# Up and gate in seven block products, the last product as a stage of its own, and w2's absolute sums through an accumulating DMA

## The reference

```
def wbin(w, base):                      # for (w1, w2, w3)
    d = w - base
    return base + mean(abs(d)) * sign(d)
xn  = layernorm(x2)                     # 1024 rows of 1024
h   = silu(xn @ wbin(w1).T) * (xn @ wbin(w3).T)   # 3584 wide
out = x2 + h @ wbin(w2).T
```

## Time and profile before

| | |
|---|---|
| median of 3 runs | 1373.06 us |
| profiled execution | span 1373.3 us (the page gives no other time for it) |
| TensorE busy | 1281.7 us (93%), 6548 matmuls recorded |
| VectorE | 816.9 us (59%) |
| ScalarE | 523.2 us (38%) |
| GpSimd | 370.7 us (27%) |
| HBM read, written | 192.27 MB, 4.19 MB |

### The profile page before, as it was taken

How to read it: one execution, slowest core, us unless ns; L and a number is a source line. 1 busy time by engine, 2 the same in 40 slices (tenths; PEclk the granted TensorE clock), 3 DMA queues, 4 the chain that set the end, 5 groups by cost and what they waited for, 6 DMA issues and landing times.

```text
span 1373.3 us, 16761 instructions
## 1 busy us (share of the span) xinstructions
PE 1281.7 (93%) x6548; PEld 1009.1 (73%) x6548; DVE 816.9 (59%) x1130; ACT 523.2 (38%) x809; POOL 370.7 (27%) x202
## 2 busy tenths in 40 slices
PE   4988787888889899999999999999999999999998
PEld 3754454556566788888888888888888888888887
DVE  6667677767778666545555554536373736454555
ACT  4776565475756454222222212131222222222220
POOL 2122232243422465222222222222222222222210
PEclk9999897789998999999999999999999999999999
DMA  7466667887210594232222323222222222223202
GB/s 286 160 241 219 229 223 268 311 313 281 109 40 17 199 375 176 94 121 93 92 93 92 103 98 107 92 92 92 92 102 101 105 92 92 93 92 118 95 33 123
DMA packets 53826, 197.55 MB, mean 144 GB/s; under 512 B 6626, under 2 KB 6900, under 8 KB 53236
## 3 DMA queue, kind: packets, MB, share of 16 engines
q1 hardware_dynamic: 53748, 196.49, 39.5%
HBM read 192.27 MB, written 4.19 MB: 143 GB/s over the span
## 4 chain that ended last, share of the span: by engine, by line
PE 80%; DVE 9%; ACT 5%; DMA 2%; issue 2%; POOL 1%; SPq 0%; DVEq 0%; ACTq 0%
PE pair L1012 39%; PE quad L1034 22%; PE pair L995 3%; DVE negwide L1446 2%; PE quad L948 2%; DMA late<-in_mean_w 2%; PE quad L958 2%; PE pair L1087 2%; PE pair L867 1%; PE pair L921 1%; PE pair L886 1%; PE pair L901 1%; POOL late L1730 1%; PE pair L1068 1%; PE quad L951 1%
## 5 line engine op out<-in xcount | busy, mean ns | idle before, releaser
L1735 POOL TENSOR_TENSOR raw_w<-raw_w,raw_base 128x1024 f32<-128x1024 f32 x84 | 213.9, 2547 | 631.1 <-DMA raw_base<-in_mean_w 631.1
L1012 PE MATMUL pair<-xnT_hi,w_hi 128*128 128x512 f32 x880 | 343.0, 390 | 1.0 <-DVE xnT_lo L1637 1.0
L1012 PE MATMUL pair<-xnT_hi,w_lo 128*128 128x512 f32 x880 | 342.5, 389 | 0.0
L1012 PE MATMUL pair<-xnT_lo,w_hi 128*128 128x512 f32 x880 | 342.4, 389 | 0.0
L1248 ACT ACTIVATE w_hi<-raw_w 128x1024 fp32r<-128x1024 f32 x84 | 89.0, 1060 | 491.2 <-DVE raw_w L1533 490.8
L1684 DVE TENSOR_TENSOR work<-sgf,pair 128x512 f32<-128x512 f32 x56 | 38.4, 686 | 281.8 <-PE pair L1012 281.8
L1012 PEld LDWEIGHTS pair<-xnT_hi,w_hi 128*128 128x128 f32 x880 | 165.3, 188 | 35.5 <-DVE xnT_lo L1637 1.4
L1012 PEld LDWEIGHTS pair<-xnT_lo,w_hi 128*128 128x128 f32 x880 | 165.3, 188 | 34.5
L1012 PEld LDWEIGHTS pair<-xnT_hi,w_lo 128*128 128x128 f32 x880 | 165.3, 188 | 34.2
L1651 DVE TENSOR_TENSOR hid<-hid,quad 128x512 f32<-128x512 f32 x208 | 139.2, 682 | 67.0 <-PE quad L1034 67.0
L1034 PE MATMUL quad<-w_hi,h_lo 128*128 128x512 f32 x416 | 161.8, 389 | 0.0
(11 more groups left out here) (239 smaller groups left out, 1569.6 us busy)
## 6 DMA issues: line engine op xcount, KB each, us to landing
raw_w<-in_w SPq DMA_DIRECT2D x84, 512.0 KB, 3.7
raw_base<-in_mean_w SPq DMA_DIRECT2D x84, 512.0 KB, 4.6
ctxw<-in_w SPq DMA_DIRECT2D x28, 512.0 KB, 4.2
ctxw<-in_mean_w SPq DMA_DIRECT2D x28, 512.0 KB, 5.3
part<-in_w SPq DMA_DIRECT2D x24, 512.0 KB, 4.0
part<-in_mean_w SPq DMA_DIRECT2D x24, 512.0 KB, 5.2
big<-in_w SPq DMA_DIRECT2D x18, 512.0 KB, 3.9
big<-in_mean_w SPq DMA_DIRECT2D x18, 512.0 KB, 5.5
```

The costliest lines, as they stand in the source:

```text
L1012: a = pe.matmul(banks[gate_bank(u, b)], ww[:, k, :], xx[:, k, :], start=k == 0 and n == 0, stop=k == KF - 1 and n == 2)
L1735: pool.tensor_tensor(w[:, :], w[:, :], base[:, :], ALU.subtract).then_inc(f_diff, 1)
```

## The change

**Seven products.** The rows are cut in the two batches, the 1024 input channels in two halves, and a pair of weight tiles (w3 and w1 of the same j) is the third cut. Instead of eight half products (2 weights x 2 batches x 2 halves, each 4 blocks x 3 matmuls) there are seven, p1 to p7, of sums of the operands. The sums of the weights are four subtractions or additions of 128x512 by VectorE (`sums_of`), written over the raw base slots; signs are, as before, written over the differences. Of the two weights 3.5 tiles of 1024 are now split, under the names d, e, f and g (g is a half), in three shared ring slots and two half slots. The sums of the rows (t1, t2, t3) are made by TensorE in phase one together with the transposes ("turn"), and t4 with 16 matmuls by an identity. The products add up in banks; ScalarE keeps snapshots of banks (sn1 to sn3), VectorE combines them (c11, c22, c21), and h is silu(c22) * x and silu(c21) * c11.

**The last product behind them.** h of each j is stored to DRAM and loaded again, twice: `step_of` takes one j and one half of the 1024 output channels, 8 row tiles x 3 matmuls of 512 columns into eight banks, which add up over all 28 j. x2 is stored to DRAM in phase one ("dump") and added once at the end of each half ("ev").

**Measuring w2.** Phase one measures only w1 and w3 (`SOON` = 56). Each tile of w2 is measured beside up and gate: SP loads the base, ScalarE negates it, a DMA issued by GpSimd adds w to it, ScalarE takes the absolute value.

```diff
-    "early": [("PE", 1.53)] * 4,
+    "dump": [("SP", 1.65)],
+    "turn": [("ACT", 1.24), ("DVE", 0.69, 0.69), ("PE", 1.5), ("PE", 2.0), ("ACT", 1.05), ("DVE", 1.22), ("ACT", 1.05),
+             ("DVE", 1.22)],
+    "early": [("PE", 1.37)] * 4,
...
-LATER, SOON = 42, 70
+LATER, SOON = 42, 2 * JT
...
+XZ, YS, SPARE = ((4, 5), (6, 7)), (2, 3), (0, 1)
+ROWS = 2 * PAIR
...
+NEED = [(which, j) for j in range(JT) for which in ("w3", "w1")]
+SLOT, FFN_HOP, AHEAD_BY = 2.72, 0.15, 0.5
+LATES, HFS, VS, RINGS, OUTS = 2, 3, 4, 3, 4
+def ffn_order():
...
+                add(("load", r), "SP", 1.0, previous("load", r), *freed, landing=4.0)
+                add(("diff", r), "POOL", 2.4, ("load", r), previous("diff", r))
+                add(("sign", r), "ACT", 1.05, ("diff", r), previous("sign", r))
+                add(("stt", r), "DVE", 1.35, ("sign", r), previous("stt", r))
...
+        add(("sn1", j), "ACT", 0.6, ("p1", j), ("c22", j - 2), previous("sn1", j))
+        add(("sn2", j), "ACT", 0.6, ("p6", j), ("c21", j - 2), previous("sn2", j))
+        add(("sn3", j), "ACT", 0.6, ("p5", j), ("c11", j), previous("sn3", j))
...
+        add(("wload", j), "SP", 0.6, ("wabs", j - LATES), previous("wload", j), landing=3.0)
+        add(("wneg", j), "ACT", 1.05, ("wload", j), previous("wneg", j))
+        add(("wadd", j), "POOL", 0.9, ("wneg", j), previous("wadd", j), landing=6.0)
+        add(("wabs", j), "ACT", 1.25, ("wadd", j), previous("wabs", j))
...
+    needs = {"p1": lambda j: (("dlo", j), ("h1", j - 2)), "p2": lambda j: (("h0", j - 2),),
+             "p6": lambda j: (("elo", j), ("sn1", j)), "p7": lambda j: (("c21", j - 2),),
+             "p5": lambda j: (("flo", j), ("sn2", j)), "p3": lambda j: (("sn3", j),),
+             "p4": lambda j: (("glo", j), ("c22", j), ("t4lo", 1))}
...
+            def product(weights, moving, bank, first, ks=range(KF // 2)):
+                (weight, at), half = weights, KF // 2
                 for k in ks:
+                    for n, (ww, xx) in enumerate(passes(weight, [moving(p, k) for p in range(2)])):
+                        a = pe.matmul(bank, ww[:, at + k, :], xx, start=first and k == 0 and n == 0,
+                                      stop=k == half - 1 and n == 2, skip_group_check=not first)
...
+            def tile_rows(n):
+                return lambda p, k: t1_b22[p][:, :, n, k, :]
...
+                elif task == "p3":
+                    pe.wait_ge(sn3, j + 1)
+                    product((ring("f", j), KF // 2), tile_rows(1), x_bank[kind], False).then_inc(products, 1)
...
+            def step_of(s):
...
+                    for n, (hh, ww) in enumerate(passes(hop[s % RINGS], vop[s % RINGS])):
+                        a = pe.matmul(banks[turn_of[t]], hh[:, t * P:(t + 1) * P], ww[:, :],
+                                      start=j == 0 and n == 0, stop=j == JT - 1 and n == 2)
...
+                elif task == "sn3":
+                    act.wait_ge(products, made["p5", j])
+                    act.wait_ge(c11, j + 1)
+                    act.activation(snap[kind][:, :], x_bank[kind], ACT.Copy).then_inc(sn3, 1)
...
+                elif task == "wabs":
+                    act.wait_ge(ld_add[n % LATES], 16 * (n // LATES + 1))
+                    act.activation(lates[n % LATES][:, :], lates[n % LATES][:, :], ACT.Abs,
+                                   accum_out=absum[:, 2, n:n + 1]).then_inc(me_abs, 1)
...
+            def sums_of(j, which):
...
+                    a = dve.tensor_tensor(found_b[:, low], wb[:, low], wb[:, high], ALU.add)
...
+                    a = dve.tensor_tensor(found_a[:, high], wb[:, low], wa[:, low], ALU.subtract)
...
+                    a = dve.tensor_tensor(found_a[:, low], wa[:, low], found_b[:, low], ALU.subtract)
...
+                    a = dve.tensor_tensor(found_b[:, high], wa[:, high], found_a[:, low], ALU.add)
...
+                elif task == "c11":
+                    dve.wait_ge(sn1, j + 1)
+                    dve.wait_ge(products, made["p2", j])
+                    dve.tensor_tensor(z_bank[kind], z_bank[kind], snap[kind][:, :], ALU.add).then_inc(c11, 1)
...
+                if task == "diff":
+                    difference(n)
+                elif task == "wadd":
+                    pool.wait_ge(w_neg, n + 1)
+                    pool.dma_start(lates[n % LATES][:, :], d["w2"][n], accum_op=ALU.add).then_inc(ld_add[n % LATES], 16)
```

1009 lines of the change are left out of this document (713 added, 296 removed).

## The result

The changed kernel took 1383.63 us, the median of 6 runs (1382.77 to 1391.52); the kernel before took 1374.32 beside it (6 runs, 1371.2 to 1376.47). The ratio is 1.0067, 95% interval 1.0036 to 1.0098: slower by 0.4 to 1.0%. The forecast was 1313, its range ended at 1350, and "slower" had a chance of 0.07. The profiled execution has a span of 1381.5 us.

What follows compares the result with a forecast made beforehand. TensorE's matmul count times 226.7 ns was taken as the bound. First products at 472, 826.9 for 3648 matmuls, 3.6 for t4, 6 of small misses and 4.5 at the end gave 1313 us, range 1298 to 1350.

Steps and rivals of the forecast that it cites:

- the turn: Switch from up/gate to the last product: waiting for loads of h and w2 costs 0 to 5 us, taken as 1.
- half time: Middle of the last product: evictions follow banks filled every 0.68 us; costs 0 to 3 us, taken as 1.
- the end: After the last product: 3.8 us as now plus 0.7 since four output buffers serve eight evictions.
- The steady count: TensorE in up/gate: 336 fewer matmuls at 226.7 ns save 76.2 us; t4 adds 3.6, net 72.5 saved.
- Rival 2: TensorE's new matmul forms take longer than 226.7 ns, up to 10 ns on all 3696: 37 us, 1348; chance 0.07.
- What must stay under cover: Other engines per 19.04 us tile: VectorE 14.6 to 17.9 us, ScalarE 11.2, GpSimd 5.1 to 7.7, DMA 193 GB/s; all fit.
- Latencies: Hand-overs in up/gate, tightest sn3 with 2.1 us to spare: small misses charged 4 us, range 0 to 56.
- Rival 1: In-order queues: VectorE runs behind the planned order, p1, p6 or sn3 wait 1 to 2 us: 39 us, 1350; chance 0.13.
- Rival 3: Accumulating DMA lands late, ScalarE's abs holds sn3 behind it; landing at 13 us costs 140 us, 1453; chance 0.08.
- One w2 tile per tile j: Work counted per tile j in up/gate: one w2 mean load and one w2 addition, within DMA's 193 GB/s.
- The start: End of phase one: first products at 472 us, range 466 to 480, with the 48 early matmuls (10.9 us) before it.

Runs made afterwards that it cites:

- r_best: Changed kernel with w2 measured by two plain loads and a VectorE subtraction, four measured VectorE durations in the plan, eight eviction buffers instead of four: 1328.06 us.
- q_costs: Changed kernel with only four of VectorE's planned durations set to the measured ones: 1345.66 us.
- n_adding_costs: Changed kernel, adding DMA kept, with four measured VectorE durations and later w2 landings (10 and 5 us) in the plan: 1340.82 us.
- v_dlo: Changed kernel with one planned duration changed, VectorE's low split of the difference 2.2 us instead of 1.3: 1348.31 us.
- e_plain: Changed kernel with GpSimd's DMA copying w2 instead of adding it, so the result is not the layer's: 1359.91 us.
- d_spread_late: Changed kernel with later planned w2 landings (10 and 5 us) and each w2 mean load tied to p1 of two tiles before: 1373.45 us.

## Why the prediction was wrong, point by point

Against the forecast the profiled execution misses by 68.5 us (1381.5 - 1313). By its own terms: matmul 133, the mark, was to start at 472 + 84 x 0.2267 + 3.6 = 494.6 and starts at 513.0 (18.4); the products and the turn were to lose 4 + 1 and lose 48.8 (43.8); half time was to cost 1 and costs 8.3 (7.3); the end 4.5, it is 3.6 (-0.9).

- **The steady count: right.** 3696 matmuls at 226.7 ns, t4 3.6 us. Rival 2 did not occur: r_best holds 2220 matmuls of all forms in their time plus 2.5 us.
- **What must stay under cover: the sums were right, the conclusion was not.** VectorE's 14.6 to 17.9 us of 19.04 never filled the slot; r_best runs dense at 84%. That a sum is below the slot says nothing of the order within it.
- **Latencies: the step that failed.** "I charge 4 us, range 0 to 56" gave sn3's room of 2.1 us correctly and named what would break it, "a wait of more than some 2 us ahead", but I did not follow what stands ahead of sn3 in ScalarE's written order. It is a w2 tile's absolute sum with an upper part and a sign (16.9 of TensorE's 32.1 us of waits), a silu that waits for c22, which in five of seven cases stands behind a split that met GpSimd (11.3 us), and a sign that waits for GpSimd (3.7 us). The term of 4 us became 48.8 with the turn's 1; with the order of q_costs the same work loses 11.1, with that of n_adding_costs 6.7. The loss lies inside the range of the term, 0 to 56, but not inside the range of the time, which ended at 1350.
- **Rival 1** (in-order queues, a plan with shorter durations than the rows) is what happened. I gave it 0.13 and 39 us, and named the wrong number, the whole weight's 1.35. The plan has 1.3 us for the split of the difference and the trace 2.52, and that one is worth 35 us (the other three, the 1.35 among them, 18). The earlier trace rows had the mechanism: 2.80 us for one instruction that met GpSimd. I used it for a sum, not for a place in the queue.
- **Rival 3** had the sign, and its mechanism in a part of the loss. ScalarE does stand for the adding DMA, 35.7 us in all, up to 6.6 at a time. The median landing is 5.6 us, but the five ahead of the waits at 595 to 769 us took 9.0 to 10.1, near the rival's 10. Wrong was that such a landing must cost 28 times what passes sn3's room: with the order of v_dlo it takes 9.9 us at the same product and costs TensorE nothing in 650 to 740. The Trainium skill, "DMA: Bandwidth & Descriptors", section "Anatomy of one DMA — SWDGE (gpsimd) path", gives 3.2 us by estimate, for a DMA without the addition. Every landing in the two kernels is longer: 5.3 us at least with the addition (the changed kernel), 3.5 without (e_plain).
- **One w2 tile per tile j: wrong.** The plan measures two, the 28 tiles within some 14 tiles j, so the larger part of the loss, 42 us, falls in 513 to 830. Spreading them alone (d_spread_late) moved the loss and did not remove it.
- **The start: wrong by 16.8 us, and 469.9 against 472 is a coincidence.** The 472 stood for the products behind the 48 early matmuls, the first p6, which starts at 488.8; what starts at 469.9 is the first early matmul. So the 48 were not hidden ahead of it (10.9 us), the last rows are turned behind it (6.2 us), and the granted clock is 0.96 in 470 to 513. The wait for sn3 ahead of the mark adds 1.2. The bank of the first product was no part of my chain; taking the bank away moved the wait. What sets the start stays open.
- **Half time: "four output buffers serve eight evictions" was charged at the end, where it costs nothing, and not at half time**, where eight buffers give back 6 to 8 us.

## What to carry to other kernels

Where an order is written out ahead from durations, put the durations that the trace shows with both engines running beside it, and look first at the instruction that stands ahead of the tightest hand-over; a single number (1.3 for 2.2 us) was worth 2.5% here. The transfer that a queue is seen to wait for is not shown to be the cause until the same transfer is kept and the order changed. Busy shares alone proved nothing in either direction: the kernel lost time at 65% and ran dense at 84%.
